# Where the expert weights of an expert layer are split into two parts, and how its first image is gated (one core)

## What is computed

```python
x = x + _L0_conv_ref(_gn(x), ...)   # norm, state-space scan of 16 states, MLP 384 -> 1536 -> 384
x = x + _L1_conv_ref(_gn(x), ...)   # four experts, the best two of each pixel
# layer 1:
scores = softmax(x_flat @ gate_w + gate_b)            # 384 -> 4, for each pixel
top_v, top_i = top_k(scores, 2); top_w = softmax(top_v)
hdn = relu(einsum('bchw,edc->ebdhw', x, w1) + b1)     # all four experts, 384 -> 384
y = einsum('ebdhw,eod->ebohw', hdn, w2) + b2          # 384 -> 384
out = einsum('ebohw,ebhw->bohw', y, coef)             # coef from top_w and the experts present
```

## Time and profile before

| what | value |
|---|---|
| time, median of 3 runs | 4130.53 us (4129.11 to 4131.14) |
| time of the profiled execution | 4128.84 us |
| its span | 4127.2 us, so 1.6 us lie around it |
| PE busy | 3808.3 us (92%) |
| DVE busy | 3366.1 us (82%) |
| ACT busy | 2660.4 us (64%) |
| POOL busy | 2647.0 us (64%) |
| mean granted TensorE clock | 0.962 of full speed |

### The profile page before, as it was taken

The page is one execution under the profiler, slowest core; times in us unless marked ns, Lnnn a source line. Parts: engine busy times, 40 slices in busy tenths (PEclk is TensorE's granted clock), DMA queues, the critical chain, the costliest instruction groups (busy, mean ns, idle before and its releaser), DMA issues.

```text
span 4127.2 us, 48978 instructions
## 1 busy us (share of the span) xinstructions
PE 3808.3 (92%) x15543; PEld 2294.7 (56%) x15543; DVE 3366.1 (82%) x4496; ACT 2660.4 (64%) x4258; POOL 2647.0 (64%) x1619
## 2 busy tenths in 40 slices
PE   6779998999998999989998999999989989999999
PEld 3444545455554545554455455545544468888887
DVE  6898989899999989998989898989999155555554
ACT  4667686867777777767776778687765334334333
POOL 1888888888888888878787888888886300000000
PEclk7789999999999999999999999999989999999999
DMA  5122222222222222222222122222222741111111
GB/s 184 44 73 64 87 74 86 77 81 73 90 65 91 76 83 98 63 95 66 93 64 90 64 87 79 88 71 90 67 85 99 273 161 41 41 41 41 41 41 36
DMA packets 155048, 336.81 MB, mean 82 GB/s; under 512 B 15900, under 2 KB 16284, under 8 KB 154308
## 3 DMA queue, kind: packets, MB, share of 16 engines
q1 hardware_dynamic: 147840, 302.19, 22.4%
q0 software_dynamic: 6224, 27.42, 1.7%
q10 hardware_dynamic: 756, 4.44, 0.3%
HBM read 298.80 MB, written 35.19 MB: 81 GB/s over the span
## 4 chain that ended last, share of the span: by engine, by line
PE 64%; DVE 16%; ACT 8%; POOL 5%; issue 5%; DMA 1%; DVEq 0%; POOLq 0%; ACTq 0%; SPq 0%
PE bank L749 12%; PE bank L900 10%; DVE hh L681 9%; PE bank L869 6%; PE bank L845 6%; PE bank L1808 6%; PE bank L1809 6%; PE bank L1810 6%; DVE yy L723 4%; PE bank L1006 3%; PE bank L821 3%; POOL vv L611 3%; PE bank L1086 2%; PE bank L1128 2%; ACT bank L653 1%
## 5 line engine op out<-in xcount | busy, mean ns | idle before, releaser
L611 POOL TENSOR_TENSOR vv<-big,bb 128x1536 f32<-128x1536 f32 x512 | 1768.2, 3454 | 515.7 <-DVE hh L681 424.8
L681 DVE TENSOR_TENSOR_SCAN hh<-bank,vv 128x512 f32<-128x512 f32 x1536 | 1847.7, 1211 | 159.8 <-ACT bank L653 102.5
L653 ACT ACTIVATE bank<-big,a_neg 128x512 f32<-128x512 f32 x1536 | 1044.5, 689 | 639.3 <-DVE hh L681 631.6
L749 PEld LDWEIGHTS bank<-ident,hh 128*128 128x128 f32 x6144 | 759.3, 146 | 1052.8 <-DVE yy L723 514.0
L749 PE MATMUL bank<-ident,hh 128*128 128x128 f32 x6144 | 1027.3, 289 | 249.9 <-DVE yy L723 158.6
L723 DVE SCALAR_TENSOR_TENSOR yy<-bank,ct,yy 128x384 f32<-128x384 f32 x1728 | 1013.6, 599 | 106.3 <-PE bank L749 101.9
L900 PE MATMUL bank<-hid,wring 128*128 128x512 f32 x1152 | 551.2, 596 | 6.5 <-ACT hid L884 6.5
L869 PE MATMUL bank<-tt,wring 128*128 128x512 f32 x1152 | 550.3, 594 | 1.5 <-issue 1.5
L1956 POOL DMA_DIRECT2D out<-xb x16 | 12.1, 754 | 840.4 <-DVE xb L1951 840.4
L1907 ACT ACTIVATE big<-bank,vv 128x512 f32<-128x512 f32 x180 | 123.7, 688 | 353.3 <-PE bank L1810 353.3
L1006 PE MATMUL bank<-xn,w_in 128*128 128x512 f32 x576 | 282.5, 607 | 2.2 <-DVE xn L994 2.2
(11 more groups left out here) (201 smaller groups left out, 4845.8 us busy)
## 6 DMA issues: line engine op xcount, KB each, us to landing
bb<-b_rows SPq DMA_DIRECT2D x512, 256.0 KB, 3.3
wring<-in_w_m SPq DMA_DIRECT2D x192, 384.0 KB, 3.1
xn<-in_x SPq DMA_DIRECT2D x16, 768.0 KB, 4.7
xr<-in_x SPq DMA_DIRECT2D x16, 768.0 KB, 6.2
x_scratch<-xr SPq DMA_DIRECT2D x16, 768.0 KB, 5.0
xb<-x_scratch SPq DMA_DIRECT2D x16, 768.0 KB, 4.5
out<-xb POOLq DMA_DIRECT2D x16, 768.0 KB, 3.9
big<-in_x SPq DMA_DIRECT2D x14, 768.0 KB, 4.5
```

What stands on the lines that cost most here:

```text
L611: product = eng.tensor_tensor(vv[:, k % 2, :, :], wu[:, js, :], bb[:, k % NBB:k % NBB + 1, :].to_broadcast([P, G3, T]), ALU.mult)
L653: e_da.inc_by(eng.activation(da[t % NDA][:, :], dt[:, j, :], ACT.Exp, scale=a_neg[:, j, n:n + 1]))
L681: e_scan.inc_by(eng.tensor_tensor_scan(hh[:, k % 2, i, :], da[(G3 * k + i) % NDA][:, :], vv[:, k % 2, i, :], 0.0, ALU.mult, ALU.add))
L749: ins = eng.transpose(ht[c % NHT][:, i * P:(i + 1) * P], hh[:, k % 2, i, c * P:(c + 1) * P], ident[:, :])
```

## The change

Four things change. (1) The split leaves layer 0: ACT and POOL no longer make parts there, `we_d` with its stores and loads is gone, and the raw weights stay in `big`. In layer 1's prologue ACT writes the high parts (`split_high`) and DVE the low parts (`split_low`) where they are used. (2) `gate_load` moves from SP's queue to POOL's, behind the constants and ahead of the raw weights; the block now ends when these have landed. (3) The rank of the experts is made in 3 comparisons and 6 updates over several experts at once, in place of 6 and 12; its four memsets go ahead of the logits, and the transposes of the logits follow the first product q = 0 on PE, not q = 1. (4) For unit 0 the coefficients are made expert by expert, each after the expert before it. The tile `land` serves as two of the buffers of the first hidden values.

```diff
-        we_d = nc.dram_tensor("expert_parts", (2 * E, 2, P, KC * C), F32).ap()
...
@@ group_stats, DVE
         dv.add(dve.tensor_tensor(tmp, tmp, mv[:, :, :, 1], ALU.add), tag + " sq")
+        if meanwhile:
+            meanwhile()
...
@@ layer0
-        def gate_load(n):
-            def sync(eng):
-                if n == 0:
-                    e_zp.wait(eng, Unit(NB - 1, 1))
-                    e_op.wait(eng, Unit(NB - 1, 0))
-                    e_st.wait(eng, Unit(EARLY - 1, 1))
+        def gate_load(eng):
+
+            e_zp.wait(eng, Unit(NB - 1, 1))
+            e_op.wait(eng, Unit(NB - 1, 0))
+            e_st.wait(eng, Unit(EARLY - 1, 1))
+            for n in range(EARLY * HALVES):
                 if n >= 4:
                     eng.wait_ge(s_egm, n - 3)
                 eng.dma_start(places[n % 4], x_half(x1_d, Unit(n // HALVES, n % HALVES)))\
                    .then_inc(s_gx[n % 4], 16)
...
-        def expert_high(q):
-            def act(eng):
...
-                if q >= 2:
-                    eng.wait_ge(s_est[q % 2], 16 * (q // 2))
-                    eng.wait_ge(s_elo, q - 1)
-                eng.activation(e_hi[q % 2].bitcast(F32R), e_raw[q], ACT.Copy).then_inc(s_ehi, 1)
...
-        def expert_low(eng, q):
-            eng.wait_ge(s_ehi, q + 1)
-            eng.dma_start(we_d[q, 0], e_hi[q % 2]).then_inc(s_est[q % 2], 16)
...
@@ layer0, POOL, after the step
-                for i, (tile, src) in enumerate(consts.weights):
-                    eng.dma_start(tile, src).then_inc(s_eraw[i], 16)
-                for q in range(2 * E):
-                    expert_low(eng, q)
-                for part in s_est:
-                    eng.wait_ge(part, 16 * E)
+                gate_load(eng)
+                for tile, src in consts.weights:
+                    eng.dma_start(tile, src).then_inc(s_const, 16)
+                eng.wait_ge(s_const, 16 * len(consts.weights))
...
@@ body, unit 0 (begun): ACT waits for all 8 splits, cf is made expert by expert
+                        eng.wait_ge(s_wlo, 2 * E)
...
-                    for e in range(E):
+                    def coef_act(e):
...
+                    for e in range(1 if begun else E):
+                        coef_act(e)
...
+                        if begun and e + 1 < E:
+                            coef_act(e + 1)
...
@@ gate_dve
             gate.aggregate(eng, dv, EARLY)
-            gate.stats(last, psum[4], dve=eng, dv=dv, ac=(s_act, 0), pc=(s_pe, 0))
+            split_low(eng, (0,))
+            gate.stats(last, psum[4], dve=eng, dv=dv, ac=(s_act, 0), pc=(s_pe, 0),
+                       meanwhile=lambda: split_low(eng, (1, 2)))
...
             gate.offset_dve(eng, dv, last, psum[6])
+            for i in range(E):
+                dv.add(eng.memset(rk[:, :, i], float(E - 1 - i)))
+            split_low(eng, range(E - 1, 2 * E - 2))
...
-            for q, (i, j) in enumerate(pairs):
-                dv.add(eng.tensor_tensor(ge[:, q, :], lg[:, :, i], lg[:, :, j], ALU.is_ge))
-            for i in range(E):
-                dv.add(eng.memset(rk[:, :, i], float(E - 1 - i)))
+            for i in range(E - 1):
+                n = E - 1 - i
+                dv.add(eng.tensor_tensor(
+                    ge[:, i, i + 1:E, :].rearrange("p j t -> p t j"),
+                    lg[:, :, i:i + 1].to_broadcast([P, NT, n]), lg[:, :, i + 1:E], ALU.is_ge))
...
             normalise(eng, "dve", 0, 1)
+            split_low(eng, (2 * E - 2, 2 * E - 1))
...
@@ gate_sync
-            load_weights(0)
...
-            for q in range(1, E):
-                load_weights(q)
             load_x1(eng, 0, 1)
-            for q in range(E, 2 * E):
-                load_weights(q)
...
+        def split_low(eng, which):
+
+            for q in which:
+                i, e = q // E, q % E
+                eng.wait_ge(s_split, q + 1)
+                eng.tensor_tensor(w_lo[i][:, e, :, :], w_raw[i][:, e, :, :],
+                                  w_hi[i][:, e, :, :].bitcast(F32),
+                                  ALU.subtract).then_inc(s_wlo, 1)
...
@@ first_mm
-                eng.wait_ge(s_w[e], 32)
+                eng.wait_ge(s_wlo, e + 1)
...
@@ gate_act
+            split_high(eng, range(E))
             gate.stats(last, psum[4], act=eng, ac=(s_act, 0), pc=(s_pe, 0))
+            split_high(eng, (E,))
             normalise(eng, "act", 0, 0)
+            split_high(eng, (E + 1,))
             for h in range(HALVES):
                 eng.wait_ge(s_gm, h + 1)
                 eng.activation(gate.glt[:, h, :], glp[h][:, 0:P], ACT.Copy).then_inc(s_gc, 1)
+            split_high(eng, (E + 2, E + 3))
             for q in range(0, 2):
                 first_relu(eng, q)
...
```

More of the change, by code:

```diff
@@ L320, in group_stats @@
 def group_stats(dve, act, pe, dv, ac, pc, mv, group, bank, tmp, gn, eps, tag, affine=False,
-                only=None):
+                only=None, meanwhile=None):
     nb = mv.shape[2]
@@ L1532, in step @@
                 st.update(gate_stages())
-                loads[("O", 0)] = [gate_load(m) for m in range(4)]
-                for m in range(4, EARLY * HALVES):
-                    loads[("G", m - 4)] = [gate_load(m)]
                 entries = list(with_gate(plan))
@@ L1759, in layer1 @@
                    [hb[:, 1, m, :] for m in range(KC)],
-                   [extra[:, KC, :], tail[:, 0, :], tail[:, 1, :]]]
+                   [extra[:, KC, :], land[:, 4 * T:5 * T], land[:, 5 * T:6 * T]]]
         gn1, lg = gate.gn, gate.lg
@@ L1782, in layer1 @@
         dv = Chain(sem("b3_dve"))
-        pairs = [(i, j) for i in range(E) for j in range(i + 1, E)]
         last = slice(EARLY, NB)
         glp, gtp = psum[4:6], psum[6:8]
-        s_w = [sem(f"expert_w{q}") for q in range(2 * E)]
+        s_wlo = sem("b3_split_low")
         def ev(name, per_unit, step=1):
@@ L1915, in body, with coef_dve @@
                 if name == "dve":
-                    for e in range(E):
+                    def coef_dve(e):
                         e_cb.wait(eng, u, e)
@@ L1920, in body @@
                             in1=cf[:, e, :], op0=ALU.mult, op1=ALU.add))
+                    if not begun:
+                        for e in range(E):
+                            coef_dve(e)
                     for e in range(E):
+                        if begun:
+                            coef_dve(e)
                         e_cf.wait(eng, u, e)
@@ L2045, in gate_sync @@
         def gate_sync(eng):
-            def load_weights(q):
-                for part, dst in enumerate((w_hi, w_lo)):
-                    eng.dma_start(dst[q // E][:, q % E, :, :].rearrange("p k c -> p (k c)")
-                                  .bitcast(F32), we_d[q, part]).then_inc(s_w[q], 16)
-            load_x1(eng, 0, 0)
-            load_weights(0)
             for h in range(HALVES):
@@ L2068, in gate_sync, with split_high @@
                 eng.wait_ge(s_gm, h + 1)
+        def split_low(eng, which):
[5 more added lines that the diff above has]
+                                  ALU.subtract).then_inc(s_wlo, 1)
+        def split_high(eng, which):
+            for q in which:
+                i, e = q // E, q % E
+                eng.activation(w_hi[i][:, e, :, :], w_raw[i][:, e, :, :],
+                               ACT.Copy).then_inc(s_split, 1)
         def first_relu(eng, q):
             e, m = q // KC, q % KC
+            if m == 0 and e:
+                eng.wait_ge(s_wlo, (E, E, E + 2, E + 2)[e])
             e_w1.wait(eng, Unit(0, 0), q)
@@ L2122, in gate_pe @@
                 gate.logits_pe(eng, glp[h], 0, last_x[h]).then_inc(s_gm, 1)
-            for q in range(0, 2):
-                first_mm(eng, q)
+            first_mm(eng, 0)
             eng.wait_ge(*marks["off"])
@@ L2128, in gate_pe @@
                 eng.transpose(gtp[h][:, 0:P], gate.glt[:, h, :], ident[:, :]).then_inc(s_gt, 1)
-            for q in range(2, 7):
+            for q in range(1, 7):
                 first_mm(eng, q)
@@ L2157, in _ @@
             def _(eng):
+                load_x1(eng, 0, 0)
                 gate_sync(eng)
```

63 lines of the change are left out of this document (23 added, 40 removed).

## The result

Over ten runs the changed kernel takes **4117.57 us** in the median (4113.43 to 4121.54), the kernel before 4130.18 us (4124.00 to 4133.72) on the same chip: a ratio of 0.9966 with a 95% interval of 0.9958 to 0.9974. That is 12.6 us less, 11 to 17 by the interval. The forecast was 4116, its range 4112 to 4122. This much of the 15.5 is no effect of the change: the constants' first products (L338) start at 3207.37 in place of 3210.08, at a point that the change does not reach (the same first products of versions with the same layer 0 start anywhere from 3206.14 to 3213.42).

The account below looks back on a forecast made before the run. PE paces the steady part, so only its earlier start counts: 8.8 us from layer 0's last step plus 4.8 from the prologue make 13.6 us; from 4128.84 and the median this gives 4115.2 and 4116.9, forecast 4116, range 4112 to 4122.

Parts of the forecast that it names:

- `hid` freed in the last step: Layer 0's last step: M2 starts 5.8 us earlier, its first products save 3.0 us of lowered clock; 8.8 us.
- rival B: Layer 0's last step: something other than ACT's queue holds `hid`, only the prologue's 4.8 us come; 4124 to 4126, chance 0.06.
- `gate_load` at zero: Layer 0's last step: moving the gating loads to POOL's queue gains and costs nothing, with 3 us of slack.
- Rival D: Last step's logits: gating loads late on POOL's queue, gain used up at 17.6 us landing; at 20 us 4134 to 4135, chance 0.03.
- The subtraction at 1.34 us: Prologue on DVE: a subtraction of 1152 elements takes 1.34 us, the first delaying the copy by 0.35 us.
- The first product 3.0 us earlier: Prologue on PE: half images no longer queue with weights and land in 4.5 us, so the first product starts 3.0 us earlier.
- W2 of the first expert 3.9 us earlier: Prologue on PE: the earlier first product plus waits of 0.60 and 0.25 us removed; 3.9 us.
- the second 4.8: Prologue on PE: the second expert's W2 starts 4.8 us earlier, 0.8 us of wait remaining; the prologue's whole gain.
- The rank at 3.4 us: Prologue on DVE: nine strided operations take 3.4 us in place of 4.9, saving 1.5 us; 3.0 at the contiguous rate.
- The coefficients, 2.05 us off DVE's path: Prologue on DVE: one coefficient instead of four ahead of the first hidden value, at 0.69 us each; 2.05 us less.
- Rival A: Prologue: subtractions at POOL's 2.63 us come onto the path, leaving 7.5 us of gain; 4121 to 4123, chance 0.09.
- rival C: Prologue: ACT's late first relus hold PE's banks back, prologue gains nothing, 8.8 us alone; 4120 to 4122, chance 0.10.

Follow-up runs that it names:

- The experiment with the copies moved: Kernel before, with ACT's weight copies q = 4 to 7 three places later, behind the second batch of `hid`: 4120.26 us against 4130.53, ratio 0.9975.
- the repeat: The changed kernel measured and profiled once more, unaltered: 4117.92 us against 4131.62 us for the kernel before.
- the one with the traffic back: Changed kernel plus 16 unused DRAM-to-DRAM transfers of 576 KB on SP's queue in the prologue: 4123.82 us against 4130.53, ratio 0.9984.
- by the experiment: Changed kernel with unit 0's coefficients made all four at once ahead of the first hidden value: 4116.79 us against 4130.53 for the kernel before.
- the doubled subtractions: Changed kernel with each of DVE's eight subtractions made twice in a row: 4121.31 us against 4130.76, ratio 0.9977.
- the one with loads on SP: Changed kernel with `gate_load` back on SP's queue at its old places: 4114.66 us against 4130.53, ratio 0.9963.
- one line: Changed kernel with the early gating's mean and variance each one stage later in layer 0's last step: 4110.60 us against 4130.76, ratio 0.9947.
- fillers: Changed kernel with six unused products on PE in the prologue's waits, meant to hold the clock up: 4116.44 us against 4130.76.

## Why the prediction was right, step by step

- **`hid` freed in the last step, 8.8 us: right.** From the constants' products to the next logits behind M2 it is 43.05 us, before 51.91 (3261.99 less 3210.08): 8.86. Of this 5.86 us are M2's earlier start and 3.0 the clock, as in the sum. The experiment with the copies moved gives 6.85 with all traffic in place and names what makes up the rest, so rival B, and with it any part of the traffic in this step beyond the stores that ACT's copies wait for, is out.
- **`gate_load` at zero: right.** 95.98 against 95.99 us to the barrier on either queue. Rival D's threshold of 17.6 us was far: the loads land in 5.5 and 6.1 us, where `xc` took 10.7. The rule of the Trainium skill ("SBUF — State Buffer", section "SBUF: two separate sides") would let each DVE operation that uses both ports hold one back. This case shows no such delay: on SP's queue the same loads landed in 5.4 and 6.1 us. But DVE was busy for only 10.3 of the 93 us from 3207 to 3300, so that is a weak test of the rule.
- **The subtraction at 1.34 us: right,** 1.35 in the mean. The first puts the copy off by 0.26 us (2.47 behind the barrier in place of 2.21), for which I had 0.35. The formula for a float32 operation on two tensors in the Trainium skill ("VectorE: DVE Perf Modes", on the errata of trn2) gives 1.36 us for 1152 elements; the trace agrees.
- **The first product 3.0 us earlier: 2.83.** The load of a half image was mis-sized: 8.1 us to landing, not 4.5. Four loads are issued within 5 us there, and the second half's logits wait 0.36 us.
- **W2 of the first expert 3.9 us earlier: 3.29; the second 4.8: 3.97.** The term that failed is the clock inside the first product. I took over its 2.9 us from before; it took 3.57 and, in the repeat, 3.65 (3320.23 to 3323.88). That is 0.7 of the missing 0.8 us. I had priced this case at up to 1.2 us more in all, but the sum took the product's time to be independent of when it starts. It is not. Read in stretches of 1 us, the clock rises 15.4 us behind the barrier in both profiles of the changed kernel, and 15.2 us in the one with the traffic back, whose first product starts at 15.1 in place of 12.4 us and takes 2.25 us. In the kernel before it was 16.4 us, with the product at 15.2. The rise did not come forward with the product, so starting earlier puts more of it on the lower clock and gives part of the gain back. With the rise ahead of the product the prologue would have gained 5.7 (50.86 against 56.59), so the forecast lies between what two profiles with the same prologue code show. The Trainium skill ("TensorE: Matmul & The Clock Gate", on what the clock gate does) says the point of the rise varies between runs. Of two profiles of one kernel these traces do not show it (15.4 us in both); over the versions with the same prologue code up to there it is 11.8 to 17.2 us behind the barrier.
- **The rank at 3.4 us: 3.0.** The price of contiguous operations, which I had rejected for strided operands, was the better one: the updates took 385, 297 and 276 ns for 192, 128 and 64 elements. But of what it saves 0.7 us arrive, since the exponential on ACT covers the rest.
- **The coefficients, 2.05 us off DVE's path:** 1.1 us of it on PE's, by the experiment.
- **Rival A** had the right price for its case (6.1 us less than the forecast's gain; the doubled subtractions cost 4.8 against the changed kernel's profile, and 6.6 against the one with loads on SP, where the first product runs at the upper clock as it does there), and **rival C** is out: PE has no wait between the first product and the 0.99 us ahead of the second W2.

The sum was 13.6 us; the traces show 8.8 and 4.0, 12.8, and the medians 12.6. The medians' own interval is 11 to 17 us, so it is the traces that bear the account out.

## What to carry to other kernels

Work that an engine does aside can still be on the path by its place in that engine's queue: look at what stands behind a copy that waits for a store, and price the gap together with the lower clock behind it. A wait to which the trace gives no releaser can be a transfer, as the 2.95 us here were; put the traffic back to find out, with no waits that were not there. Work that is brought forward into a stretch at the lower clock gains less than it moves: 1.4 of 2.7 us here. And before a wait for data is covered with more work, see whether the stage that waits can simply come one stage later: one line brought half as much again as the change had.

## What the runs showed of the hardware

- The granted clock fell to 0.50 between 0.4 and 3.5 us behind the barrier in the versions without fillers, and rose 11.8 to 17.2 us behind it (worked out from the stretches of 1 us in which it changed); the same prologue code took 50.9 or 52.6 us up to the second W2, depending on whether the rise came ahead of the first product.
- PE kept busy with its own small products (one column wide) and with fillers (384 columns) between them did not keep the clock: 2.90 of 3.00 us busy, and 0.72 falling to 0.50.
- A wait of 0.93 us ahead of M2 left the clock at 1.00; one of 5.79 did not the earlier trace rows. A wait of 2.9 us for the constants was followed by products at the lower clock (7.09 us for twelve, 5.40 without the wait).
- A transfer of 768 KB landed in 5.5 us on POOL's queue and 5.4 us on SP's with little beside it, and in 8.1 us on SP's with others issued right around it.
